# Row scatters of the last routing block in an expert-tile loop: which tiles carry them, and which transposes release them

## The chip, the core and the metric

One core of a Trainium2 chip runs the whole kernel. The metric is the device time of one execution in microseconds (us); smaller is better. Engines are named as in the profile: PE is TensorE, DVE is VectorE, ACT is ScalarE, POOL is GpSimd, SP is SyncE. PEld is PE's loading of weights.

## The reference

One decoder layer on 32 sequences of 64 tokens with 256 features: self-attention, cross-attention on a context, and a mixture of experts. The changed code belongs to the last part:

```python
probs = jax.nn.softmax(x @ Wr, axis=-1)            # x: layernorm of the residual, 2048 x 256
topk_w, topk_idx = jax.lax.top_k(probs, 2)         # 2 of 8 experts
topk_w = topk_w / jnp.sum(topk_w, axis=-1, keepdims=True)
output = jnp.zeros_like(x)
for i in range(8):
    w_i = jnp.sum(topk_w * (topk_idx == i), axis=-1, keepdims=True)
    h = silu(x @ Wg[i]) * (x @ Wu[i])
    output = output + w_i * (h @ Wd[i])
x = x + output
```

## The kernel before

Five instruction streams, one per engine, run side by side and meet through semaphores. The 2048 tokens are handled in four blocks of 512 (16 token tiles of 128). After cross-attention, each block is routed: layernorm, logits, the two best experts, and a slot for each of the two choices. POOL then writes the 128 normed rows of a token tile to their slots in HBM by `scatter(b, n)`: an indirect DMA from `mxhat` to `slots`, one for each of 4 tiles and 2 choices, so `n` runs over 0 to 7 (line 1829).

Rows for the experts are gathered in two parts. Part 0 holds blocks 0 to 2 and has 31 expert tiles; part 1 holds block 3 and has 15. The loop over these 46 tiles is the last large stage of the kernel. Block 3 is routed within it while the tiles of part 0 are computed: its slots are made in iteration `ROUTE_LAST["slots"]` = 14.

In iteration i, with mm3 standing for three matmuls (high by high, high by low, low by high), PE does in this order: `gate_up(i)`, 6 matmuls into `bank`; `h_T(i-1)`, two transposes of `gu`, which update `t_hT`; `down(i-2)`, 6 matmuls; `x_T(i+2)`, two transposes of `xs`, which update `t_xT`. ACT does `silu(i)` (`sg`), `h_high(i-1)` (`thh`), `copy_out(i-2)` (`ys`), `x_high(i+2)` (`txh`). DVE does `gated(i)` (`gu`), `h_low(i-1)` (`thl`), `x_low(i+2)` (`txl`), `places(i+2)` (`place`). POOL does `store(i)` (line 1863): it waits for `place` and for `ys` of tile i, and scatters 128 result rows to HBM by an indirect DMA. The four `ys` buffers are reused after that store has landed. SP issues `load(i+6)` (line 1941), which waits for `x_T(i+2)` and `places(i+2)`; the four `xs` buffers are reused this way.

The expert tiles of part 1 need all rows of block 3: `load(31)` waits until `d_scat` shows all eight scatters landed. Then SP reads the table's rows into registers and issues the DMA. Loads stand in one order on SP, so loads 32 and up wait behind load 31. `x_T(31)`, in iteration 29 of PE, is the first to read part 1.

All scatters and stores of POOL are in one order on its queue. The loop around the change is the end of `gpsimd` (lines 1866 to 1873); the rest of its waits are in `scatter` and `store`.

Of the kernel before, what the change touches and what calls it, by code (L numbers as in the profile page):

```python
# [147 lines left out]
def decoder(nc, a, const_dram, const_at, out):  # L148
    with ExitStack() as ctx:
# [144 lines left out]
        slots = [nc.dram_tensor(f"slots{i}", (ROWS[i], D + 2), F32, kind="Internal").ap() for i in range(2)]  # L294
# [41 lines left out]
        t_xT, t_xh, t_xl, t_proj, t_silu, t_gu, t_hT, t_hh, t_hl, t_down, t_y, t_comb, t_place = (  # L336
            sem("t_xT"), sem("t_xhigh"), sem("t_xlow"), sem("t_proj"), sem("t_silu"), sem("t_gu"), sem("t_hT"), sem("t_hhigh"),
            sem("t_hlow"), sem("t_down"), sem("t_y"), sem("t_comb"), sem("t_place"))
# [15 lines left out]
        ROUTE_LAST = {"stats": 0, "norm": 2, "T": 4, "logits": 6, "max": 6, "exp": 8, "rank": 9, "pos": 13, "slots": 14}  # L354
# [1406 lines left out]
        def gpsimd(e):  # L1761
            w = Waits(e)
# [61 lines left out]
            def scatter(b, n):  # L1824
                q = int(b == 3)
                t, k = divmod(n, 2)
                w.wait_ge(r_route, RK * b + 25)
                w.wait_ge(d_fill, 32)
                e.indirect_dma_start(out=slots[q][:, :], out_offset=bass.IndirectOffsetOnAxis(ap=index[:, 4 * b + t, k:k + 1], axis=0),
                                     in_=mxhat[:, t, :], in_offset=None).then_inc(d_scat, 16)  # L1830
# [29 lines left out]
            def store(i):  # L1860
                w.wait_ge(t_place, i + 1)
                w.wait_ge(t_y, i + 1)
                e.indirect_dma_start(out=results[:, :], out_offset=bass.IndirectOffsetOnAxis(ap=place[:, i:i + 1], axis=0),  # L1863
                                     in_=ys[i % 4][:, :], in_offset=None).then_inc(d_ys[i % 4], 16)

            route_step(3, 0, ROUTE_LAST)
            for i in range(sum(TILES)):
                n = i - ROUTE_LAST["slots"]
                if 0 <= n < 8:
                    w.wait_ge(t_xT, ROUTE_LAST["slots"] + 4 + n)  # L1870
                    scatter(3, n)
                store(i)
            e.drain().then_inc(s_phase, 1)

# [103 lines left out]
        with nc.Block() as block:  # L1978
            block.tensor(tensor)
            block.vector(vector)  # L1980
            block.scalar(scalar)
            block.gpsimd(gpsimd)
            block.sync(sync)
# [35 lines left out]
```

## Time and profile before

| | us |
|---|---|
| median of 3 runs | 705.26 (703.32 to 705.65) |
| profiled execution, whole | 705.3 |
| its span, first to last instruction | 703.3 |
| PE busy / DVE / ACT / POOL | 640.8 / 501.9 / 348.9 / 256.0 |
| mean granted PE clock | 0.964 |

The span is what the trace covers; 2.0 us of the profiled execution lie around it. Times in the rows below count from the start of the span. A row of the timeline gives start, duration, engine, line, operation and tiles, and in brackets how long the engine was idle before it and which instruction ended that wait. "remote" means that the trace doesn't show who ended it, and "issue" that it shows no wait that ended then. Line 359 is the helper that records every matmul, and line 368 the one for transposes, so one has to go by tiles: `whi,txl` closes gate_up, `whi,thl` closes down, `cst,gu` is h_T and `cst,xs` is x_T.

### The profile page before, as it was taken

The page shows a single profiled execution, that of the slowest core. Times are in us where ns is not written, and L with a number is a line of the kernel's source. Part 1 is how long each engine was busy: PE and PEld are TensorE (multiplying, and loading weights), DVE is VectorE, ACT ScalarE, POOL GpSimd, SP SyncE. Part 2 cuts the span into 40 slices and gives each one's busy share as a digit, 9 for nine tenths or more (in the row PEclk, how much of TensorE's full clock was granted, in tenths as well). Part 3 has the DMA queues.
Part 4 walks back from the last instruction along what each step waited for, and adds up shares of the span by engine and source line. Part 5 has one row for each costly group of instructions (what it writes and reads, how often), then busy time and mean ns, then how long its engine had stood idle before and what let it go on. Part 6 is the DMA issues. An engine that isn't in the chain of part 4 may idle for free.

```text
span 703.3 us, 15360 instructions
## 1 busy us (share of the span) xinstructions
PE 640.8 (91%) x5650; PEld 477.3 (68%) x5650; DVE 501.9 (71%) x1210; ACT 348.9 (50%) x1207; POOL 256.0 (36%) x233
## 2 busy tenths in 40 slices
PE   3787999998899999999999999999988999889991
PEld 2566777767787657676677675776645688768881
DVE  5897999977467688548885498845887956534575
ACT  1476999978580116702176013651258546434541
POOL 2113000000006646624277542865517023453332
PEclk9998999987899999999999999999989999999997
DMA  8799970000000000000000300012081223333457
GB/s 294 167 358 340 333 268 1 3 1 2 1 3 16 15 1 3 1 16 1 3 1 17 106 1 1 1 40 69 1 259 66 62 83 99 114 106 106 124 183 248
DMA packets 42008, 61.77 MB, mean 88 GB/s; under 512 B 15280, under 2 KB 36272, under 8 KB 41328
## 3 DMA queue, kind: packets, MB, share of 16 engines
q1 hardware_dynamic: 36528, 49.23, 22.9%
q0 software_dynamic: 3744, 10.26, 3.9%
q10 hardware_dynamic: 1664, 1.31, 0.7%
q8 instruction: 46, 0.75, 0.4%
q14 instruction: 26, 0.21, 0.1%
HBM read 48.44 MB, written 31.38 MB: 113 GB/s over the span
## 4 chain that ended last, share of the span: by engine, by line
PE 76%; ACT 8%; DVE 7%; issue 3%; DMA 3%; another core or an unknown queue 1%; SPq 1%; POOL 0%; POOLq 0%; ACTq 0%; DVEq 0%
PE bank L359 65%; PE bank L368 11%; DMA wkv_s<-in_L_xattn_w_kc_kv 2%; ACT kbd L1543 2%; ACT vbd L1529 1%; DVE wlo L1400 1%; SPq L1883 1%; ACT ex L1553 1%; ACT xth L1509 1%; DVE x L1466 1%; ACT ex L1669 1%; DMA gb<-results 0%; DVE m L1119 0%; DVE xhat L1359 0%
## 5 line engine op out<-in xcount | busy, mean ns | idle before, releaser
L1119 DVE TENSOR_TENSOR m<-bank,cst 128x512 f32<-128x512 f32 x192 | 122.0, 684 | 38.4 <-PE bank L359 37.1
L1815 POOL TENSOR_TENSOR r<-m,m 128x512 f32<-128x512 f32 x80 | 104.5, 1331 | 114.9 <-DVE m L1119 95.1
L1669 ACT ACTIVATE ex<-bank,nmax 128x64 f32<-128x64 f32 x256 | 73.2, 337 | 27.2 <-DVE nmax L1366 27.1
L359 PE MATMUL bank<-xth,wbh 128*128 128x512 f32 x192 | 79.9, 416 | 1.1 <-DVE m L1119 1.1
L359 PE MATMUL bank<-xth,wbl 128*128 128x512 f32 x192 | 75.2, 392 | 0.0
L359 PE MATMUL bank<-xtl,wbh 128*128 128x512 f32 x192 | 75.1, 391 | 0.0
L1863 POOL DMA_INDIRECT results<-ys,place x46 | 44.4, 964 | 74.8 <-ACT ys L1742 72.2
L1652 ACT ACTIVATE qc<-bank 128x512 f32<-128x512 f32 x32 | 17.4, 595 | 102.9 <-PE bank L359 102.9
L359 PE MATMUL bank<-wop,qc 128*128 128x256 f32 x256 | 62.5, 389 | 0.2 <-DVE x L1395 0.2
L359 PE MATMUL bank<-r,wqk 64*64 64x512 f32 x512 | 57.7, 594 | 0.0
L359 PEld LDWEIGHTS bank<-wop,qc 128*128 128x128 f32 x256 | 46.4, 189 | 15.5 <-issue 9.1
L1553 ACT ACTIVATE ex<-bank,nmax 128x64 f32<-128x64 f32 x256 | 54.3, 360 | 1.6 <-DVE nmax L1021 1.5
L1669 ACT ACTIVATION_READ_ACCUMULATOR ex<-bank,nmax 128x1 f32 x216 | 49.5, 230 | 0.0
L359 PEld LDWEIGHTS bank<-xth,wbh 128*128 128x128 f32 x192 | 36.0, 188 | 19.0 <-issue 10.1
L1780 POOL TENSOR_TENSOR x<-x,borow 128x512 f32<-128x512 f32 x8 | 10.1, 1270 | 105.0 <-DVE xhat L953 78.7
L1835 POOL TENSOR_TENSOR ex<-ex,inv 128x512 f32<-128x512 f32 x32 | 33.4, 1044 | 41.0 <-DVE inv L1376 40.6
L368 PE MATMUL bank<-cst,ex 128*128 128x128 f32 x256 | 42.6, 292 | 5.6 <-ACT ex L1553 3.3
L1455 DVE TENSOR_TENSOR gu<-bank,sg 128x256 f32<-128x256 f32 x46 | 19.4, 422 | 33.5 <-ACT sg L1732 29.5
L368 PEld LDWEIGHTS bank<-cst,ex 128*128 128x128 f32 x256 | 30.2, 147 | 19.0 <-issue 8.7
L359 PE MATMUL bank<-whi,txh 128*128 x92 | 40.5, 441 | 2.7 <-issue 1.8
L1732 ACT ACTIVATE sg<-bank 128x256 f32<-128x256 f32 x46 | 17.7, 386 | 49.1 <-PE bank L359 27.1
L359 PEld LDWEIGHTS bank<-xth,wbl 128*128 128x128 f32 x192 | 36.0, 188 | 8.1
(222 smaller groups left out, 1517.7 us busy)
## 6 DMA issues: line engine op xcount, KB each, us to landing
slots<-in_fill SPq DMA_DIRECT2D x1, 13416.0 KB, 52.3
xs<-slots SPq DMA_DIRECT2D x46, 129.0 KB
slots<-in_fill SPq DMA_DIRECT2D x1, 5160.0 KB, 61.8
gb<-results SPq DMA_DIRECT2D x16, 256.0 KB
wo_s<-in_L_xattn_Wo SPq DMA_DIRECT2D x1, 2048.0 KB, 17.6
wq_s<-in_L_xattn_Wq SPq DMA_DIRECT2D x1, 2048.0 KB, 11.8
wraw<-in_L_ffn_Wg SPq DMA_DIRECT2D x8, 256.0 KB, 3.7
wraw<-in_L_ffn_Wu SPq DMA_DIRECT2D x8, 256.0 KB, 3.9
```

Source lines behind the costliest of these rows:

```text
L359: return e.matmul(o, l, r, start=start, stop=stop, skip_group_check=True)
L368: last = e.transpose(o, i, ident)
L1119: last = e.tensor_tensor(m4[n % 2][m][:, :].rearrange("p (b s) -> p b s", s=S), products[half][:, :].rearrange("p (b s) -> p b s", s=S), t ...
L1455: e.tensor_tensor(gu[i % 2][:, :], bank[1 + i % 2][:, F:2 * F], sg[i % 2][:, :], ALU.mult).then_inc(t_gu, 1)
L1543: last = e.activation(kbd[p2][:, :, 2 * t:2 * t + 2, 64 * h2:64 * h2 + 64], bank[0][:, 256:512].rearrange("p (t b l) -> p t b l", t=2, b=2 ...
L1553: last = e.activation(ex[u][:, h * 64:(h + 1) * 64], bank[3 + u % 2][:, h * 64:(h + 1) * 64], ACT.Exp, bias=nmax[u][:, h:h + 1], scale=1.0)
L1652: e.activation(qc[:, 2 * g + pair, :], latent_banks(blk, g)[pair][:, :], ACT.Copy).then_inc(c_qb, 1)
L1669: last = e.activation(ex[b % 4][:, h * 64:(h + 1) * 64], score_banks(b)[odd][:, n * 64:(n + 1) * 64], ACT.Exp, bias=nmax[b % 4][:, 4 * odd ...
L1732: e.activation(sg[i % 2][:, :], bank[1 + i % 2][:, 0:F], ACT.Silu).then_inc(t_silu, 1)
L1815: last = e.tensor_tensor(rope[n % 6][half][:, :], m4[n % 2][first][:, :], m4[n % 2][second][:, :], op)
L1835: e.tensor_tensor(segments(ex[b % 4]), segments(ex[b % 4]), per_head(inv[b % 2]), ALU.mult).then_inc(c_exn, 1)
L1863: e.indirect_dma_start(out=results[:, :], out_offset=bass.IndirectOffsetOnAxis(ap=place[:, i:i + 1], axis=0), in_=ys[i % 4][:, :], in_offs ...
```

## The change

Before, the iterations 14 to 21 of POOL's loop each issue one scatter of block 3 ahead of their store. The scatter of iteration i waits for `x_T(i+3)`, the last step of PE's iteration i+1. After, the iterations 14, 15, 17, 18, 20, 21, 23 and 24 issue one each, and 16, 19 and 22 none. The scatter of iteration i waits for `h_T(i+1)`, which PE does in iteration i+2 between gate_up and down. Scatters, stores and their order among themselves are the same otherwise.

```diff
             route_step(3, 0, ROUTE_LAST)
             for i in range(sum(TILES)):
-                n = i - ROUTE_LAST["slots"]
-                if 0 <= n < 8:
-                    w.wait_ge(t_xT, ROUTE_LAST["slots"] + 4 + n)
-                    scatter(3, n)
+                t, half = divmod(i - ROUTE_LAST["slots"], 3)
+                if 0 <= t < 4 and half < 2:
+                    w.wait_ge(t_hT, i + 2)
+                    scatter(3, 2 * t + half)
                 store(i)
             e.drain().then_inc(s_phase, 1)
```

## Rows read from the trace of the kernel before

**Rows 1.** The page: busy time by engine, and shares of the chain that ended last.
```profile
PE 640.8 (91%) x5650; PEld 477.3 (68%) x5650; DVE 501.9 (71%) x1210; ACT 348.9 (50%) x1207; POOL 256.0 (36%) x233
...
PE 76%; ACT 8%; DVE 7%; issue 3%; DMA 3%; another core or an unknown queue 1%; SPq 1%; POOL 0%; POOLq 0%; ACTq 0%; DVEq 0%
```

**Rows 2.** Windows: each engine's busy us, PE clock, DMA share, GB/s.
```profile
600.00:620.00 20.00, 17.53 (x110) 14.99 (x109) 11.26 (x43) 8.71 (x27) 11.10 (x13) 1.00 0.39 121
620.00:640.00 20.00, 17.14 (x98) 14.79 (x97) 8.40 (x26) 8.29 (x25) 8.39 (x10) 0.91 0.34 105
640.00:660.00 20.00, 19.03 (x121) 16.51 (x120) 9.30 (x29) 9.79 (x30) 7.57 (x8) 1.00 0.30 93
```

**Rows 3.** Timeline of POOL, scatters and stores of the changed stretch.
```profile
601.82 0.96 POOL L1863 DMA_INDIRECT results<-ys,place  x1 [1.58 <-ACT ys L1742]
603.08 0.96 POOL L1829 DMA_INDIRECT slots<-mxhat,index  x1 [0.30 <-issue]
...
605.62 0.96 POOL L1829 DMA_INDIRECT slots<-mxhat,index  x1 [0.31 <-issue]
608.99 0.96 POOL L1863 DMA_INDIRECT results<-ys,place  x1 [2.41 <-ACT ys L1742]
...
627.50 0.96 POOL L1829 DMA_INDIRECT slots<-mxhat,index  x1 [0.31 <-issue]
```

**Rows 4.** Timeline of POOL, two stores after the changed stretch, five tiles apart.
```profile
634.79 0.96 POOL L1863 DMA_INDIRECT results<-ys,place  x1 [1.59 <-ACT ys L1742]
...
647.56 0.96 POOL L1863 DMA_INDIRECT results<-ys,place  x1 [1.60 <-ACT ys L1742]
```

**Rows 5.** Timeline of ACT: ys of tiles 13, 19 and 22, and two long waits.
```profile
600.68 0.38 ACT L1742 ACTIVATE ys<-bank 128x256 f32<-128x256 f32 x1 [0.27 <-PE bank L359]
...
606.85 0.38 ACT L1732 ACTIVATE sg<-bank 128x256 f32<-128x256 f32 x1 [2.98 <-issue]
...
618.79 0.38 ACT L1742 ACTIVATE ys<-bank 128x256 f32<-128x256 f32 x1 [0.27 <-PE bank L359]
...
624.55 0.38 ACT L1732 ACTIVATE sg<-bank 128x256 f32<-128x256 f32 x1 [3.96 <-remote]
...
631.10 0.38 ACT L1742 ACTIVATE ys<-bank 128x256 f32<-128x256 f32 x1 [0.27 <-PE bank L359]
```

**Rows 6.** Timeline of PE: x_T and h_T, then the last matmul of two gate_up.
```profile
600.48 0.38 PE L368 MATMUL bank<-cst,xs 128*128 128x128 f32 x2
602.09 0.38 PE L368 MATMUL bank<-cst,gu 128*128 128x128 f32 x2
604.40 0.40 PE L359 MATMUL bank<-whi,txl 128*128 x1
...
619.97 0.40 PE L359 MATMUL bank<-whi,txl 128*128 x1
```

**Rows 7.** Windows: 2.5 us after ACT's longest wait; columns as in rows 2.
```profile
625.00:627.50 2.50, 1.63 (x8) 1.66 (x9) 2.04 (x6) 1.43 (x5) 0.95 (x1) 0.66 0.00 0
```

**Rows 8.** Timelines, an earlier block: its last scatter on POOL; DVE behind PE.
```profile
392.14 0.96 POOL L1829 DMA_INDIRECT slots<-mxhat,index  x1 [0.30 <-issue]
...
394.64 0.42 DVE L1395 TENSOR_TENSOR x<-bank,x 128x256 f32<-128x256 f32 x1 [2.13 <-remote]
```

**Rows 9.** Timelines of PE, DVE, SP: h_T(25), place(27), load(31), x_T(31); chain: last store.
```profile
635.07 0.38 PE L368 MATMUL bank<-cst,gu 128*128 128x128 f32 x2
...
634.68 0.21 DVE L1450 SCALAR_TENSOR_TENSOR place<-xs,own 128x1 uint32<-128x1 f32 x1
...
637.07 0.95 SPq L1941 DMA_DIRECT2D xs<-slots  x2
...
643.66 0.38 PE L368 MATMUL bank<-cst,xs 128*128 128x128 f32 x2
...
690.67 2.81 DMA results<-ys,place
```

**Rows 10.** Waits from 634 to 647, stores alone: total us, times, longest us.
```profile
ACT sg L1732 <- issue: 3.9, 4, 1.0
```

## The prediction

> **What bounds the kernel now.** I read the page first. PE is busy for 91% of the span and carries 76% of the chain that ended last; POOL carries none of it [rows 1]. So a scatter on POOL costs something only if it disturbs PE. The windows show where that happens: in the 20 us after the change's stretch PE is busy for 19.0, in the two before it for 17.5 and 17.1 [rows 2]. These two hold all eight scatters, from 603.08 to 627.50 [rows 3].
>
> How much is lost there comes from a count of tiles. Past the stretch, five tiles take 647.56 - 634.79 = 12.77 us, or 2.55 each [rows 4]. ACT's copies of the results are the cleanest mark of a tile, since each follows PE's down at once. From that of tile 13 to that of tile 19 pass 618.79 - 600.68 = 18.11 us where 6 x 2.55 = 15.30 would do: 2.8 us lost beside the first four scatters. From tile 19 to 22 pass 12.31 where 7.65 would do: 4.7 lost beside the last four [rows 5]. Together 7.5 us, and this is all that the change can win.
>
> What the loss is made of: POOL is nearly full here. A store begins at 601.82, and scatters at 603.08 and 605.62 with a store between them [rows 3], so each DMA takes 1.26 to 1.27 us of POOL, and two of them 2.54 of the 2.55 us of a tile. Then ACT waits twice for long, for 2.98 and 3.96 us, and no instruction is named that ended these waits [rows 5]. PE's rows show the matmuls that ACT waits for as long done: gate_up ended at 604.80 and its silu began at 606.85; gate_up ended at 620.37 and its silu began at 624.55 [rows 5, 6]. The word that PE was done came 2.0 and 4.2 us late. I call this a hold. It isn't peculiar to this loop: in an earlier block too scatters follow each other with 0.30 us between, and just behind the last of them DVE waits 2.13 us with no one named [rows 8]. Beside single stores 2.55 apart [rows 4] the longest wait of silu is 1.0, part of the tile's rhythm [rows 10]. So I take the holds as an effect of indirect DMAs that follow each other at 1.26 us, three or more of them; that is read from their coincidence, and nothing in this trace proves it.
>
> After the longest hold, in which PE ran dry, the granted clock is 0.66 of full in a window of 2.5 us, so most of it is at 1.2 and the rest at 2.4 GHz [rows 7]. That is part of the 4.7.
>
> **The change, part by part.** Nothing is added or removed: eight scatters of 0.96 us remain [rows 3]. Three things move.
>
> 1. The later release. x_T ends at 600.86, and the h_T that now counts ends at 602.47 [rows 6], 1.6 us later. A store begins 0.76 us after its copy ends (601.82 - 601.06) [rows 3, 5]; with that wake-up the first scatter begins at 602.47 + 0.76 = 603.23 instead of 603.08. Behind the waiting scatter stands the store of the same tile, and behind that store the reuse of its ys buffer four tiles on. By the rhythm of a tile that store is due at 601.82 + 2.55 = 604.37 and must now wait until 603.23 + 1.27 = 604.50, so it is 0.13 us late, with three tiles of cover. Cost nothing, hidden under PE; without that cover it would be 0.13 us a scatter, 1.0 in all.
>
> 2. The same wait as a brake. Before, a scatter waited for something long past, so POOL went on issuing into a hold: that at 605.62 began while word from PE was late. Now h_T's update comes from PE itself, in mid-tile; when it is held, the next scatter and all of POOL behind it stay back too. What lies in flight then is one DMA less, and a hold should be shorter. No row shows a hold after only three DMAs, so I bound its price. From above: the first four scatters, two pairs with a gap of 2.4 us between them on POOL (606.58 to 608.99, [rows 3]), cost 2.8 us, 1.4 a pair. From below: nothing, as beside single stores [rows 4]. I take 1.1, nearer the upper end, because store 13, scatter, store 14 stand as before to within 0.15 us, and that is where the first hold begins.
>
> 3. Two tiles in three. A run is now store, scatter, store, scatter, store, five DMAs, and then POOL has 2.55 - 0.96 = 1.6 us without one. There are four such runs. The last four scatters no longer form one run in which holds build up to 4 us, and without such a hold PE's clock shouldn't fall.
>
> Sum: 4 x 1.1 = 4.4 us where 7.5 were, so 3.1 us less.
>
> 4. The last scatter is later, and load 31 waits for it. Counted by the trace of before, h_T(25) ends at 635.45; the scatter begins at 636.2; the last store of the kernel, as many rows of nearly the same size, took 2.81 us from issue to landing, which puts it at 639.0 [rows 9]. SP then reads its registers: place ended at 634.89 and the DMA was issued at 637.07, 2.2 us [rows 9]. That gives an issue at 641.2. For the load no row shows a landing; with the 2.81 of the store, an upper value since a load needs no work of POOL, the rows are there by 644.0, and x_T(31) begins at 643.66 [rows 9]. This is the one place with thin cover: 0.3 us short with two upper values, and 0.7 to spare if the load takes the 2.81 less POOL's 0.96 of issuing. I take nothing, and keep up to 1 us for the upper end. Loads 32 and up follow at once, and each has a tile more of time.
>
> **The rivals.**
>
> A. The holds cost per run what a pair costs now: 4 x 1.4 = 5.6, so 1.9 us less: 703.4. For it: the first hold begins at the third DMA, and all four runs have three. Against it: the brake above.
>
> B. With the brake and the gap the holds all but vanish, at 0.4 a run: 1.6 instead of 7.5, so 5.9 less: 699.4. For it: single stores cost nothing. Against it: runs of five remain.
>
> C. The change does nothing for the time, because the holds are not made by the scatters: 705.3, give or take 0.9. The DMA share of the core is 0.39 and 0.34 in these windows, far from full [rows 2], and the rows name no culprit. Against it: both long waits of ACT stand beside scatters, and none stands beside stores alone [rows 5, 10]. The Trainium skill (SBUF — State Buffer, Who interferes with whom) states that DMA never contends with a compute engine. By that rule the late word from PE has another source and this rival is the result; the rows just named speak against the rule, without refuting it.
>
> D. Slower. The release in mid-tile puts each scatter's transfer under the end of the next gate_up, and the hold that caught gate_up beside a full queue was the longest, 4.2 us late. If every run now meets such a hold, each costs what the last four scatters lost but for the clock. The clock, 0.91 over 20 us [rows 2], took at most 20 x 0.09 = 1.8 of the 4.7; 2.9 a run are left, 11.6 in all, 4.1 more than now. For it: the releases of all eight scatters now fall into that phase. Against it: the long run that stood around that hold is gone. It decides from (7.5 + 2.1) / 4 = 2.4 a run; halfway between that and 2.9, 10.6 in all, the time is 708.4.
>
> **How the numbers follow.** The sum is made on the profiled execution of 705.3 us, which is the median, 705.26, to within a tenth. Forecast: 705.3 - 3.1 = 702.2. Chances: the forecast 0.40, A 0.24, B 0.12, C 0.12, D 0.12. The range 699.2 to 706.8 takes in the forecast, A, B but for its lower tail, and C; D and the tails are left out. About 0.3%, 2.1 us, is what a measurement of this kernel can tell from no change: faster is below 703.1, slower above 707.4. The forecast lies below for 0.34 of its 0.40, B wholly, A for 0.08: 0.54 faster. Slower is D but for a little, 0.11. The rest, 0.35, is same.
>
> **What would show it.** Right: POOL shows four runs of five DMAs at 1.26 us with a pause of about 1.6 between; ACT's waits in the stretch are under 2 us; no window there has a clock below 1.0; ys of tile 13 to ys of tile 25 takes 30.6 + 4.4 = 35.0 us. Step 1 is wrong if a store waits for its scatter for over 0.2 us. Step 2 is wrong if a hold goes on while no scatter is in flight. Step 4 is wrong if x_T(31) waits for its load. The forecast falls if waits over 2.5 us are still there after each run (A or D), or if they move to tiles without a scatter (C).

## The result, and the profile after

The change made the kernel faster: 698.54 us (696.30 to 701.34, 10 runs) beside 703.68 us for the kernel before (701.27 to 705.65, 10 runs); the ratio is 0.9926, with a 95% interval of 0.9907 to 0.9944. That is 5.1 us between the medians where 3.1 were forecast, and it lies 0.7 us below the range. The profiled execution of after took 701.3 us, its span 699.4.

The windows of the kernel after, columns as in rows 2:

```profile
600.00:620.00 20.00, 20.00 (x128) 17.42 (x127) 13.21 (x51) 10.53 (x32) 10.69 (x11) 1.00 0.44 120
620.00:640.00 20.00, 20.00 (x127) 17.29 (x126) 10.65 (x32) 10.71 (x33) 11.52 (x12) 1.00 0.44 130
640.00:660.00 20.00, 19.02 (x118) 16.41 (x117) 9.77 (x30) 9.46 (x29) 6.88 (x8) 1.00 0.38 110
```

PE is now busy for all of the 40 us in which it had 17.5 and 17.1 of 20, and the clock of the second window is 1.00 instead of 0.91 [rows 2]. The third is as it was. So the time came out of the stretch with the scatters. Behind it nothing was given back: from the store of tile 25 to the last store pass 50.89 us, where the kernel before has 50.78.

POOL in the kernel after: one whole run of the new schedule (five DMAs), the first store of the next run, and further on the store of tile 25:

```profile
604.69 0.96 POOL L1863 DMA_INDIRECT results<-ys,place  x1 [1.60 <-ACT ys L1742]
605.95 1.07 POOL L1829 DMA_INDIRECT slots<-mxhat,index  x1 [0.30 <-issue]
607.33 0.96 POOL L1863 DMA_INDIRECT results<-ys,place  x1 [0.30 <-issue]
609.27 0.96 POOL L1829 DMA_INDIRECT slots<-mxhat,index  x1 [0.98 <-PE bank L368]
610.53 0.96 POOL L1863 DMA_INDIRECT results<-ys,place  x1 [0.30 <-issue]
612.54 0.96 POOL L1863 DMA_INDIRECT results<-ys,place  x1 [1.04 <-ACT ys L1742]
...
635.60 0.96 POOL L1863 DMA_INDIRECT results<-ys,place  x1 [0.85 <-ACT ys L1742]
```

The first row is the store of tile 13, the last that of tile 25. Between them lie 30.91 us. In the trace of the kernel before the same two stores are 38.07 apart (601.82 [rows 3] to 639.89); twelve tiles of 2.55 would be 30.6. The loss of 7.5 us is down to 0.3. The second scatter of the run waited 0.98 us for h_T, named here as PE at line 368, instead of the usual 0.30: the brake at work. From ys of tile 13 to ys of tile 25 pass 30.92 us (603.54 to 634.46), where the forecast named 35.0.

ACT in the kernel after, with PE's last matmul of the gate_up that each silu waits for:

```profile
602.18 0.40 PE L359 MATMUL bank<-whi,txl 128*128 x1
602.62 0.38 ACT L1732 ACTIVATE sg<-bank 128x256 f32<-128x256 f32 x1 [0.97 <-PE bank L359]
...
607.30 0.39 PE L359 MATMUL bank<-whi,txl 128*128 x1
608.25 0.38 ACT L1732 ACTIVATE sg<-bank 128x256 f32<-128x256 f32 x1 [1.49 <-PE bank L359]
...
614.93 0.40 PE L359 MATMUL bank<-whi,txl 128*128 x1
616.04 0.39 ACT L1732 ACTIVATE sg<-bank 128x256 f32<-128x256 f32 x1 [1.63 <-PE bank L359]
```

The word of PE still comes late after the third DMA of a run, but by 0.56 and 0.71 us (607.69 to 608.25, 615.33 to 616.04), and by 0.78 and 0.62 in the other two runs, not by 2.0 and 4.2 [rows 5, 6]. Before a run it takes 0.04. A delay of 0.7 us fits into what PE has queued ahead: it is busy for 20.00 of 20 us here. One of 2 us did not: in the kernel before PE went on through down, x_T and the next gate_up until 607.34 and then stood for 1.23 us, since ACT and DVE had given it nothing new:

```profile
606.94 0.40 PE L359 MATMUL bank<-whi,txl 128*128 x1
608.57 0.41 PE L368 MATMUL bank<-cst,gu 128*128 128x128 f32 x2 [1.23 <-DVE thl L1459]
```

The holds are still there, cut short.

### The profile page after: what moved, and what is told of

It is laid out like the page before. It is cut to its first block, busy times and chain, and to the rows that moved or that the text cites. A ratio compares the mean times of both kernels' runs of the same rounds, so it can differ in the third digit from the quotient of the medians.

```text
span 699.4 us, 15360 instructions
## 1 busy us (share of the span) xinstructions
PE 641.6 (92%) x5650; PEld 476.7 (68%) x5650; DVE 502.2 (72%) x1210; ACT 349.7 (50%) x1207; POOL 256.3 (37%) x233
## 3 DMA queue, kind: packets, MB, share of 16 engines
q0 software_dynamic: 3744, 10.26, 4.0%
## 4 chain that ended last, share of the span: by engine, by line
PE 79%; ACT 8%; DVE 7%; issue 3%; DMA 2%; POOL 0%; ACTq 0%; SPq 0%; POOLq 0%; DVEq 0%
PE bank L359 68%; PE bank L368 11%; ACT kbd L1543 2%; ACT vbd L1529 1%; DMA lncol<-in_L_attn_ln_kv_b 1%; DVE wlo L1400 1%; ACT ex L1553 1%; ACT xth L1509 1%; DMA gb<-results 1%; ACT ex L1669 1%; DVE m L1119 0%; DVE xhat L1359 0%; DMA results<-ys,place 0%; DVE x L1466 0%; ACT wbh L1599 0%
## 5 line engine op out<-in xcount | busy, mean ns | idle before, releaser
L359 PEld LDWEIGHTS bank<-xtl,wbh 128*128 128x128 f32 x192 | 36.1, 188 | 6.5
L359 PEld LDWEIGHTS bank<-r,wqk 64*64 64x64 f32 x512 | 18.7, 133 | 31.7 <-issue 31.7
```

Source lines behind the costliest of these rows:

```text
L359: return e.matmul(o, l, r, start=start, stop=stop, skip_group_check=True)
```

## The experiments

There were seventeen further runs, in six groups, each group on one chip beside the kernel before. The chips turned out to be of two sorts, and that has to be known to read the rest. On four of them the kernel before took 703.4 to 704.2 us, and all traces show late words of PE, in this loop or in the earlier blocks; on two it took 696.0 and 696.2, and in all eight traces each silu of the changed stretch begins 0.03 to 0.05 us after PE's last matmul. The first comparison, 703.7, was of the first sort. I call a chip with holds a late chip, one without a prompt chip. No chip was used for two groups, so the runs can't tell a lasting property of a chip from a condition of the time at which its group ran.

The clearest measure is the distance in a trace from the store of tile 13 to that of tile 25. Whole times are less clear, because the time up to the loop moves by several us with the same code: on the first prompt chip store 13 begins at 596.25 in the changed kernel and at 604.35 in the one without scatters, and the difference is there long before any changed line (377.91 and 385.96 at the first addition of the first routed block). The granted clock differs there too, 0.93 and 0.86 from 50 to 100 us.

| kernel | late chips: ratio (interval) | stores 13 to 25 | prompt chips: ratio (interval) | stores 13 to 25 |
|---|---|---|---|---|
| before | 0.9996 (0.9978 to 1.0015) | 38.0, 38.1 | 1 | not traced |
| spacing alone | 0.9961 (0.9946 to 0.9976) | 35.2 | 1.0004, 0.9988 | 30.8 |
| release alone | 0.9904 (0.9882 to 0.9926), 0.9966 (0.9944 to 0.9988) | 33.9, 34.0 | 1.0009 (0.9995 to 1.0022) | 30.8 |
| changed | 0.9926 (0.9907 to 0.9944), 0.9940 (0.9919 to 0.9961) | 30.9, 31.6 | 1.0005, 0.9978 (0.9955 to 1.0000) | 30.8 |
| no scatter | 0.9893 (0.9850 to 0.9936) | 30.6 | 0.9996, 0.9995 | 30.6 |
| plain DMA instead | 0.9914 (0.9881 to 0.9946) | 30.6 | 1.0000 (0.9982 to 1.0017) | 30.6 |
| compute instead | 0.9991 (see below) | 32.0 | not run | |
| changed, earlier scatters apart too | 0.9926 (0.9898 to 0.9955) | 31.8 | not run | |

The kernel before was not traced on a prompt chip; that it has no holds there is read from its time, which is that of its variants. A late chip costs it 7 to 8 us: 7.2 of them lie between the two stores (38.0 against the 30.8 of all kernels with scatters on prompt chips), the rest in the earlier blocks.

**The two halves of the change, first on a prompt chip.** Spacing alone keeps the old release:

```diff
-                    w.wait_ge(t_hT, i + 2)
+                    w.wait_ge(t_xT, i + 4)
```

> Spacing alone: two scatters in three tiles as in the change, each released by x_T(i+3) as before. The changed kernel's ratio to the kernel before is 0.9926, 5.2 us. Theory B (the brake: the release in mid-tile keeps POOL from issuing into a late update of PE): at most 2 us of the gain, ratio 0.997 to 1.000, and waits of ACT over 2 us still in the trace. Rival S (the spacing does it: one tile in three without a scatter ends the run of DMAs): nearly the whole gain, ratio 0.992 to 0.994.

Release alone keeps one scatter in each of the tiles 14 to 21:

```diff
-                    w.wait_ge(t_xT, ROUTE_LAST["slots"] + 4 + n)
+                    w.wait_ge(t_hT, i + 2)
```

> Release alone: a scatter in each of the tiles 14 to 21 as before, each released by h_T(i+1) as in the change. Theory B: at least 3 us of the gain, ratio 0.992 to 0.996. Rival S: nothing or a little, ratio 0.998 to 1.002, with waits of ACT of 2 to 4 us as before.

> The changed kernel itself, on the same chip as the two halves of the change: ratio 0.991 to 0.995 under every theory. It is the anchor against which the halves are read.

No scatter leaves out the whole block with `scatter(3, ...)`, load 31 waits for `128 * 3`, and the last four token tiles read result rows of the first four:

> The floor: no scatter of block 3 at all, so the expert tiles of part 1 compute on filler rows; load 31 waits for the scatters of the first three blocks only, and the last four token tiles combine rows of the first four, so that no unwritten row is read. Output left wrong for the last block. If the scatters make the late updates, ACT has no wait over 1.8 us between tiles 13 and 22 and the ratio is 0.989 to 0.992 (7.5 us less at most by the trace of before, 5.2 to 7.5 expected). If the late updates have another source, the ratio is 0.998 to 1.002.

Measured: 1.0004, 1.0009, 1.0005 and 0.9996, with the kernel before at 696.03 us (35 runs). Neither theory was right, since there was nothing to gain here, not even by leaving the scatters out. POOL of release alone on this chip:

```profile
598.25 0.96 POOL L1863 DMA_INDIRECT results<-ys,place  x1 [1.58 <-ACT ys L1742]
599.51 0.96 POOL L1829 DMA_INDIRECT slots<-mxhat,index  x1 [0.30 <-issue]
600.79 0.96 POOL L1863 DMA_INDIRECT results<-ys,place  x1 [0.32 <-issue]
602.05 0.96 POOL L1829 DMA_INDIRECT slots<-mxhat,index  x1 [0.30 <-issue]
603.33 0.96 POOL L1863 DMA_INDIRECT results<-ys,place  x1 [0.32 <-issue]
604.60 0.96 POOL L1829 DMA_INDIRECT slots<-mxhat,index  x1 [0.31 <-issue]
605.88 0.96 POOL L1863 DMA_INDIRECT results<-ys,place  x1 [0.32 <-issue]
607.14 0.96 POOL L1829 DMA_INDIRECT slots<-mxhat,index  x1 [0.30 <-issue]
```

It goes on like this for sixteen DMAs. ACT's silus beside it, with PE's last matmul for the third of them:

```profile
601.27 0.38 ACT L1732 ACTIVATE sg<-bank 128x256 f32<-128x256 f32 x1 [0.95 <-PE bank L359]
603.81 0.38 ACT L1732 ACTIVATE sg<-bank 128x256 f32<-128x256 f32 x1 [0.96 <-PE bank L359]
605.93 0.40 PE L359 MATMUL bank<-whi,txl 128*128 x1
606.37 0.38 ACT L1732 ACTIVATE sg<-bank 128x256 f32<-128x256 f32 x1 [0.97 <-PE bank L359]
608.93 0.38 ACT L1732 ACTIVATE sg<-bank 128x256 f32<-128x256 f32 x1 [0.97 <-PE bank L359]
```

They are 2.54 to 2.56 us apart, and the third begins 0.04 us after PE's matmul ends (606.33 to 606.37), so no word is late. The brake never bites, because each h_T is long seen when POOL comes to its scatter. So the density of the DMAs is not enough to make a hold; it takes a late chip too.

**Is it the chip, or the kernel?** The kernel before with a trace of its own, and release alone:

> The kernel before once more, now with a trace of its own on the chip of this call. In the first comparison it took 703.7 us and its trace had late updates of PE beside the scatters; beside the four runs so far it took 696.0 us, and none of their traces has a late update, not even where eight scatters follow each other in eight tiles. Theory H (the late updates come and go with the chip or its surroundings, and only where they come do the scatters' places matter): this trace has either both, a time near 704 and ACT waits over 2 us between tiles 13 and 22 as well as DVE waits of 2.1 us and more behind the scatters of the earlier blocks, or neither, with a time near 696. Rival N (the late updates belong to the kernel before on any chip, and the changed kernel and the halves are free of them): waits in the loop here too, while the time is near 696.

> Release alone again (a scatter in each of tiles 14 to 21, released by h_T(i+1)), next to the kernel before. Theory H: ratio 1.000 within 0.002 if the kernel before shows no late updates in this call; if it shows them, 0.992 to 0.997 by the brake, or 0.999 to 1.001 if spacing alone is what helps. Rival N: ratio below 0.996 in any case.

Measured on the second chip: 703.47 and 704.11 us for two sets of runs of the kernel before, so theory H holds, in its wide form (the chip or its surroundings), and N falls. Release alone had 0.9904, a little below the 0.992 to 0.997 expected. The earlier blocks, whose code no variant but one touches, tell the two sorts apart in every trace. DVE's two additions behind the scatters of the first block in the kernel before on this late chip:

```profile
387.15 0.42 DVE L1395 TENSOR_TENSOR x<-bank,x 128x256 f32<-128x256 f32 x1
393.11 0.42 DVE L1395 TENSOR_TENSOR x<-bank,x 128x256 f32<-128x256 f32 x1 [2.09 <-remote]
```

and in release alone on the prompt chip:

```profile
385.82 0.41 DVE L1395 TENSOR_TENSOR x<-bank,x 128x256 f32<-128x256 f32 x1
389.56 0.42 DVE L1395 TENSOR_TENSOR x<-bank,x 128x256 f32<-128x256 f32 x1 [1.14 <-PE bank L359]
```

5.96 us apart on the one and 3.74 on the other: 2.2 us of hold with the same instructions. Most of it is made good there before the block ends. The waits for no one named, of which rows 8 show one, are on all late chips and on neither prompt one; the one kernel on a late chip that lacks them is the one with those scatters moved (below).

The brake in release alone on the late chip, where it does bite (POOL, then ACT and the last matmul that its long wait is for):

```profile
621.99 0.96 POOL L1829 DMA_INDIRECT slots<-mxhat,index  x1 [1.20 <-remote]
623.26 0.96 POOL L1863 DMA_INDIRECT results<-ys,place  x1 [0.30 <-issue]
624.52 0.96 POOL L1829 DMA_INDIRECT slots<-mxhat,index  x1 [0.30 <-ACT ys L1742]
625.79 0.96 POOL L1863 DMA_INDIRECT results<-ys,place  x1 [0.30 <-issue]
628.08 0.95 POOL L1829 DMA_INDIRECT slots<-mxhat,index  x1 [1.34 <-remote]
```

```profile
625.07 0.40 PE L359 MATMUL bank<-whi,txl 128*128 x1
627.80 0.38 ACT L1732 ACTIVATE sg<-bank 128x256 f32<-128x256 f32 x1 [3.25 <-remote]
```

POOL stops at every second scatter for 1.2 to 1.3 us, but between the stops it gets four DMAs out, and the word of PE is then 2.3 us late (625.47 to 627.80). The brake takes the loss from 7.4 us to 3.3 over the floor of 30.6; it doesn't end it.

**Once more, for a late chip.** The third group was on a prompt chip again:

> Spacing alone again, hopefully on a chip that shows late updates (whether it does is read from DVE's waits behind the scatters of the first block, 2.1 to 2.8 us or none, before the changed code is reached). The kernel before takes 38.0 us from store 13 to store 25 there, release alone 33.9, the changed kernel 30.9 in its first trace. Theory B (the brake is what helps most): 36 to 38 us, ratio 0.997 to 1.001. Rival S (each half alone takes the holds away in good part): 31 to 34 us, ratio 0.990 to 0.995. On a chip without late updates: 30.8 us, ratio 1.000.

> The changed kernel beside spacing alone: with late updates on this chip, 30.9 us between the two stores and a ratio of 0.990 to 0.994 under every theory; without, 30.8 us and 1.000.

> No scatter of block 3 (the rest as in e4_none; output left wrong for the last block). With late updates in the earlier blocks of this trace: 30.6 us between the stores and no ACT wait over 1.8 us there if the scatters cause them, ratio 0.988 to 0.992; over 33 us if they come from elsewhere. Without late updates on this chip: ratio 1.000.

The fourth kernel of that group is the kernel before with a plain DMA of POOL, to a tensor of its own, in place of each scatter (the lines that set up the tensor and the last tiles' reads are left out here):

```diff
-                    w.wait_ge(t_xT, ROUTE_LAST["slots"] + 4 + n)
-                    scatter(3, n)
+                    w.wait_ge(t_xT, i + 4)
+                    w.wait_ge(r_route, RK * 3 + 25)
+                    e.dma_start(plain[P * n:P * n + P, :], mxhat[:, n // 2, :]).then_inc(d_scat, 16)
```

> As no scatter, but at the eight places of the kernel before POOL issues a plain DMA of the same 128 rows of 1032 bytes to a scratch tensor in HBM (load 31 waits for these; output left wrong for the last block). If late updates come from POOL's DMAs of any kind at 1.26 us (theory Q), about 38 us between the stores, as before. If it takes the indirect ones (theory I: row by row descriptors, data-dependent addresses), 30.6 to 31.5 us.

Measured: 0.9988, 0.9978, 0.9995 and 1.0000, the kernel before at 696.21 us. They show that the first prompt chip was not the only one, and nothing else.

**Spacing alone and the floor, on a late chip.**

> Spacing alone, once more in search of a chip that shows late updates (two of the four so far did: kernel before near 704 us; two did not: near 696). If DVE waits 2.1 us or more behind the scatters of the first two blocks, then theory B (the brake helps most) expects 36 to 38 us from store 13 to store 25 and a ratio of 0.997 to 1.001; rival S (spacing alone takes a good part) 31 to 34 us and 0.990 to 0.995. If not: 30.8 us and 1.000.

> No scatter of block 3 (the rest as in e4_none; output left wrong for the last block). If the earlier blocks of this trace show late updates: 30.6 us between the stores and a ratio of 0.988 to 0.992 if scatters make them; over 33 us if not. Without late updates on this chip: ratio 1.000.

Spacing alone: 35.2 us between the stores and 0.9961, between what theory B and rival S had named, so spacing gives 2.8 of the 7.4 us. Its first hold is as long as ever, as the forecast had it for the change: gate_up ended at 604.65 and the silu began at 606.73.

```profile
604.25 0.40 PE L359 MATMUL bank<-whi,txl 128*128 x1
606.73 0.38 ACT L1732 ACTIVATE sg<-bank 128x256 f32<-128x256 f32 x1 [3.00 <-remote]
```

Without scatters the same chip has the twelve tiles in 30.62 us and the ratio 0.9893, while the first block's hold is there in the same trace:

```profile
386.01 0.41 DVE L1395 TENSOR_TENSOR x<-bank,x 128x256 f32<-128x256 f32 x1
392.02 0.42 DVE L1395 TENSOR_TENSOR x<-bank,x 128x256 f32<-128x256 f32 x1 [2.14 <-remote]
```

No silu of that stretch is over 0.04 us behind PE. That shows that on a late chip the scatters make the holds. Rival C of the prediction falls with it. The ratio rests on four executions.

**What kind of work makes them.**

> As e10_direct: no scatter, but a plain DMA of POOL with the same rows at the eight places of the kernel before (output left wrong for the last block). Read only if this chip shows late updates behind the scatters of the first two blocks. Theory Q (POOL's DMAs of any kind make them): about 38 us from store 13 to store 25. Theory I (only indirect ones do): 30.6 to 31.5 us.

Measured on a late chip (first block's wait for no one: 2.11 us): 30.63 us from store to store, 0.9914. POOL:

```profile
604.55 0.96 POOL L1865 DMA_INDIRECT results<-ys,place  x1 [1.58 <-ACT ys L1744]
605.51 0.60 POOL L1874 DMA_DIRECT2D plain<-mxhat  x1
607.10 0.98 POOL L1865 DMA_INDIRECT results<-ys,place  x1 [0.99 <-ACT ys L1744]
608.09 0.57 POOL L1874 DMA_DIRECT2D plain<-mxhat  x1
```

The same rows, the same bytes, from the same queue (3744 packets and 10.26 MB on POOL's queue in both kernels), and no hold: ACT's longest wait there is 1.0 us, and each silu begins 0.03 to 0.05 us after PE's last matmul. Theory I holds. The plain DMA also takes POOL only 0.6 us, so this run doesn't tell the indirect addressing from the longer work on POOL. The next one was to (only the loop is shown; load 31 and the last tiles' reads are as in no scatter):

```diff
-                    w.wait_ge(t_xT, ROUTE_LAST["slots"] + 4 + n)
-                    scatter(3, n)
+                    w.wait_ge(t_xT, i + 4)
+                    w.wait_ge(s_pad, n)
+                    e.tensor_tensor(mxT[:, 0, 0:384], mxT[:, 1, 0:384], mxT[:, 1, 0:384], ALU.add).then_inc(s_pad, 1)
```

> No scatter, but at its eight places a tensor_tensor of POOL of 128x384 from SBUF to SBUF, about 1 us, as long as a scatter's issue (the rest as no scatter; output left wrong for the last block). If late updates show behind the scatters of the earlier blocks: a POOL kept busy between stores is enough if it takes about 38 us from store 13 to store 25; it takes the indirect DMA itself if it is 30.6 to 31.5 us, which I expect after e13_direct.

Its time, 0.9991, says nothing: the wait for the last logits that I put ahead of the loop, so that PE is done with `mxT`, held the first store back to 576.1, and ACT stood for 5.0 us for want of a ys buffer. That was my mistake. Its stretch can be read: the twelve tiles took 31.96 us on a late chip, outside both ranges expected, but no wait of ACT in it is over 1.0 us and each silu begins 0.03 to 0.04 us after PE's last matmul, so there is no hold. The 1.3 us over the floor lie at 608 to 615 and have another cause (below, on the hardware). A busy POOL alone makes no hold: POOL had a store and a tensor_tensor of 0.83 us in each of eight tiles.

**The earlier blocks.**

```diff
-            SCATTER_AT = [{7: (0,), 8: (1,), 9: (2, 3), 10: (4, 5), 11: (6, 7)}] * 3 + [{3: (0,), 4: (1,), 5: (2, 3), 6: (4,), 7: (5, 6), 8: (7,)}]
+            SCATTER_AT = [{7: (0,), 8: (1,), 9: (2,), 10: (3,), 11: (4,), 12: (5,)}] * 3 + [{3: (0,), 4: (1,), 5: (2, 3), 6: (4,), 7: (5, 6), 8: (7,)}]
...
+                    if blk > 1 and n == 6:
+                        scatter(blk - 2, 6)
+                        scatter(blk - 2, 7)
                     rope_sums(blk, n)
```

> The changed kernel, and in the first two routed blocks too the eight scatters apart: one in each step from 7 to 12 and the last two after the context's work, instead of seven back to back. On a chip with late updates the changed kernel loses, beside the scatters of these two blocks, waits of DVE of 2.1 us each that one without late updates has not: if these go too, it is 2 to 4 us faster than the changed kernel, ratio to the kernel before 0.985 to 0.991. On a chip without: 0.999 to 1.001; slower by over 1 us anywhere if the later scatters hold up the next block's norm.

Measured on a late chip: 0.9926 (0.9898 to 0.9955), no better than the changed kernel. The waits for no one named are gone, and the additions of the first block stand as on a prompt chip, 3.74 us apart:

```profile
384.67 0.41 DVE L1395 TENSOR_TENSOR x<-bank,x 128x256 f32<-128x256 f32 x1
388.41 0.42 DVE L1395 TENSOR_TENSOR x<-bank,x 128x256 f32<-128x256 f32 x1
```

The plain-DMA kernel, on the same chip, has them 5.85 apart (391.63 to 397.48). So the early holds come from the scatters too, but they cost little. From the first addition of the first routed block to that of the next pass 83.99 us, as on prompt chips, where the other late traces have 84.18 to 84.40; the same distance one block on is 74.42, where they have 74.59 to 74.78. That is 0.4 to 0.7 us in all, not 2 to 4. I had taken waits for loss; most of them were made good within the block. In the loop it had 31.8 us.

**Release alone against the whole change, on one late chip.**

> The changed kernel beside release alone on one chip. With late updates: 30.9 to 31.8 us from store 13 to store 25, ratio 0.989 to 0.993. Without: 1.000.

> Release alone. With late updates: 33 to 34.5 us between the same stores, so 2 to 3 us slower than the changed kernel. Without: 1.000, 30.8 us.

Measured: the changed kernel 0.9940 and 31.58 us between the stores, release alone 0.9966 and 34.04. So 2.5 us separate the stretches and 2.0 the medians, as expected; the 0.9940 is just above the 0.989 to 0.993 expected. The intervals of release alone from the two late chips, 0.9882 to 0.9926 and 0.9944 to 0.9988, don't even touch, while its two traces agree, 33.92 and 34.04. So these ratios are less sure than their intervals say, and the price is better read from the traces. The late words of the changed kernel on this chip are 0.58, 0.82, 0.16 and 1.47 us: the brake doesn't cut every hold to the same length.

## Why the prediction was wrong in size

The sign, the place and the mechanism were right; the size was not. Point by point:

- **The loss** of 7.5 us and its place held: leaving the scatters out gives 7.4 us in the trace (38.0 to 30.6) and a ratio of 0.9893, which is 7.5 us.
- **Holds as an effect of indirect DMAs following each other** was argued from coincidence, and the runs show it, with two limits that the trace of before couldn't show: only on some chips, and only by indirect ones. That holds can be there or not with the same kernel is the largest fact that the prediction lacked. On a prompt chip rival C's number is right, though not its reason.
- **Step 1**, the later release, costs nothing: right, but the 0.13 us by its own working did not come. The h_T that counts, h_T(15), ended at 605.36, and the scatter began at 605.95, 1.26 after the store, held back by nothing; the wake-up of 0.76 us was not needed. The store behind it was due at 604.69 + 2.55 = 607.24 and began at 607.33, 0.09 us late, because the scatter took 1.07 us instead of 0.96. That the two numbers are close is luck.
- **Step 2**, the price of a run, is the step that failed: 1.1 us was taken, and (30.91 - 30.62) / 4 = 0.07 measured, on another late chip (31.58 - 30.62) / 4 = 0.24. I had put it near the upper end because the first three DMAs stand as before, and took the start of a hold for its size. The start is the same, a late word after the third DMA. What the size depends on is what POOL issues next. In spacing alone, where POOL issues the next scatter at once, the word is 2.1 us late; in the change, where that scatter waits for a late word itself, it is 0.56 and, on the other chip, 0.58 us. I read this as a feedback, and the prediction treated it as one DMA less. So 4 x 1.1 = 4.4 us of loss were forecast where 0.3 and 1.0 were measured.
- **Step 3**, two tiles in three, was right in direction. Spacing without the brake gives 2.8 us, the brake without spacing 4.1 (38.00 - 33.92), both together 7.2 in the first traces and 6.5 on the last chip. So the two about add up (6.9). A reading of it that no run tests is that each ends the run of DMAs at another point: the brake ahead of the second scatter of a run, the gap behind its last store. The form of the run was wrong: not five DMAs at 1.26 us but three, a pause of 0.98, and two, and then not 1.6 us of pause but 1.0.
- **The clock** stayed at 1.00 in the windows, as forecast.
- **Step 4**, load 31: it was issued at 637.26, 4.74 us after the last scatter began; 5.0 had been worked out (636.2 to 641.2). x_T(31) began at 639.37, 2.57 us after x_T(30), by the rhythm of a tile, so the load was hidden.
- **The base.** The sum stood on an execution of 705.3 us, which was high for this kernel: ten runs have a median of 703.68. That is 1.6 of the 3.7 us by which the forecast was too high; the other 2.0 are gain beyond the 3.1 us that step 2 had left. Rival B, the right one, was priced at 699.4 from that base, with 0.4 a run; with the measured base and price it would have been 703.7 - 7.2 = 696.5, and the median of after, 698.5, lies between. So it is partly luck that B came within 0.9 us. Why the medians differ by 5.1 us where the two stretches differ by 7.2 stays open: the interval of the ratio ends at 6.5 us, so the spread of the ten runs does not cover it, and the two traces can't say, since store 13 already comes 2.87 us later in the one of after.
- **Rival D** never came: where every scatter was released in mid-tile and no tile was spared, the worst word was 2.3 us late, and the kernel was still faster than before.

Open: why some chips are late, or were so when they were used. No row names what holds the word of PE back, and the traces of both sorts differ in nothing else that I found. It is PE's word that is late and not one engine that wakes late: ACT, DVE [rows 8] and POOL (the 1.20 and 1.34 us in release alone) all wait for PE in this way. The semaphore updates that the traces record, which the views don't print, say the same: h_T(16) of the kernel before ended at 605.01 and its update is recorded at 607.56, where h_T(15), ahead of the hold, has 0.02 us between the two. Also open is which part of an indirect DMA does it, its addresses from a table or its longer work on POOL, 0.96 us against 0.6; the plain DMA changed both.

## What to carry to other kernels

If an engine waits for work that another has long finished by its own rows, look at what a third one issues beside it: here the cure was no faster instruction but fewer indirect DMAs in a row. Let a burst that can delay an engine wait for that engine's own progress: here it throttled itself where it hurt (4.1 us less) and cost nothing where it didn't (30.8 us either way). Measure such a change on more than one chip: on two of the chips here it is worth nothing, on the others 0.6 to 0.7%.

## What the runs showed of the hardware

- Indirect DMAs of POOL at 1.26 us each delayed the updates of PE's finished matmuls on four of six chips and not at all on the other two; the longest delay, in the kernel before, was 4.2 us. The Trainium skill (SBUF — State Buffer, Who interferes with whom) states that DMA never contends with a compute engine. For plain DMAs the runs agree (30.63 us with, 30.62 without); for indirect ones on late chips they don't, and the measurement decides. What is contended for stays unknown. PE's matmuls themselves kept their pace: in the first hold of the kernel before they go on until 607.34, while ACT waits until 606.85 for one that ended at 604.80.
- A tensor_tensor of POOL with inputs in SBUF stretched DVE instructions beside it. DVE and POOL in the kernel with compute work:

```profile
606.14 1.32 DVE L1288 TENSOR_TENSOR upto<-cst,ntile 128x64 f32<-128x64 f32 x1
606.54 0.84 POOL L1873 TENSOR_TENSOR mxT<-mxT 128x384 f32<-128x384 f32 x1
...
609.03 0.94 DVE L1450 SCALAR_TENSOR_TENSOR place<-xs,own 128x1 uint32<-128x1 f32 x1
609.11 0.83 POOL L1873 TENSOR_TENSOR mxT<-mxT 128x384 f32<-128x384 f32 x1
```

  `upto` takes 0.23 us in the kernel before (at 602.41) and `place` 0.21 [rows 9]; the inputs of both are in SBUF. The same section of the Trainium skill says that DVE with two inputs in SBUF contends with a GpSimd instruction that reads SBUF; the trace agrees, with 1.09 us for `upto`, 0.73 for this `place` and 0.52 for the next, while POOL's instruction keeps its 0.83. These three are the only ones stretched, and the silus behind them, at 611.70 and 615.05, come 3.14 and 3.35 us after the one before instead of 2.55: 1.4 us, which is the stretch's excess over the floor.
